# Opening of a two-layer kernel: tables fetched later, warm-up matmuls, an earlier T1, and the experts' table in two parts

## The reference

```python
gate = lora_add(einsum('bnh,fh->bnf', x, W_gate), x, A_gate, B_gate)   # F = 2752, rank 16, 16 adapters
up   = lora_add(einsum('bnh,fh->bnf', x, W_up),   x, A_up,   B_up)
act  = silu(gate) * up
y    = lora_add(einsum('bnf,hf->bnh', act, W_down), act, A_down, B_down)
logits = y @ W_gate + b_gate                       # 8 experts, other weights than above
_, top_idx = top_k(logits, 2)
out = x + mean(relu(einsum('bsd,edh->bseh', y, W_e) + b_e) taken at top_idx, over the two)
```

## Time and profile before

| | |
|---|---|
| median of 3 runs | 1841.7 us (1838.97 to 1843.03) |
| profiled execution, its time | 1838.5 us |
| its span | 1836.6 us |
| PE busy | 1808.3 us (98%) |
| DVE busy | 1255.6 us (68%) |
| ACT busy | 754.8 us (41%) |
| POOL busy | 1097.3 us (60%) |
| moved by DMA | 350.34 MB, mean 191 GB/s |

### The profile page before, as it was taken

How to read it: one execution, slowest core, us unless ns; L and a number is a source line. 1 busy time by engine, 2 the same in 40 slices (tenths; PEclk the granted TensorE clock), 3 DMA queues, 4 the chain that set the end, 5 groups by cost and what they waited for, 6 DMA issues and landing times. The chain is left out here.

```text
span 1836.6 us, 25207 instructions
## 1 busy us (share of the span) xinstructions
PE 1808.3 (98%) x8578; PEld 1505.3 (82%) x8578; DVE 1255.6 (68%) x1489; ACT 754.8 (41%) x1197; POOL 1097.3 (60%) x712
## 2 busy tenths in 40 slices
PE   8999999999999999999999999999999999999997
PEld 6788888888888888888888888888888888888886
DVE  7977887885567797888888886477798743234400
ACT  5544444443543335444443444443323333333332
POOL 3788888873444454446656543444434777777674
PEclk9999999999999999999999999999999999999999
DMA  6466566645577655555566565576635875567653
GB/s 227 161 232 222 207 205 224 240 138 172 194 247 245 220 186 169 189 179 180 189 205 210 187 205 191 192 255 221 223 109 188 246 195 149 145 188 194 150 104 48
DMA packets 128973, 350.34 MB, mean 191 GB/s; under 512 B 15296, under 2 KB 17216, under 8 KB 128576
## 3 DMA queue, kind: packets, MB, share of 16 engines
q1 hardware_dynamic: 110608, 286.92, 45.6%
q0 software_dynamic: 17952, 61.75, 14.1%
q10 hardware_dynamic: 288, 0.02, 0.0%
HBM read 267.49 MB, written 90.05 MB: 195 GB/s over the span
## 5 line engine op out<-in xcount | busy, mean ns | idle before, releaser
L1831 PE MATMUL PS<-R,ring 128*128 128x512 f32 (+1 forms) x1804 | 708.5, 393 | 11.0 <-DVE R L1022 8.4
L1832 PE MATMUL PS<-R,ring 128*128 128x512 f32 (+1 forms) x1804 | 704.0, 390 | 0.0
L1833 PE MATMUL PS<-R,ring 128*128 128x512 f32 (+1 forms) x1804 | 703.5, 390 | 0.0
L1831 PEld LDWEIGHTS PS<-R,ring 128*128 128x128 f32 x1804 | 339.7, 188 | 79.2 <-DVE ring L956 11.6
L1833 PEld LDWEIGHTS PS<-R,ring 128*128 128x128 f32 x1804 | 339.3, 188 | 71.8
L1832 PEld LDWEIGHTS PS<-R,ring 128*128 128x128 f32 x1804 | 339.8, 188 | 66.0
L824 POOL TENSOR_TENSOR ring<-raw,ring 128x1024 fp32r<-128x1024 f32 x78 | 192.2, 2464 | 268.9 <-ACT ring L963 268.8
L803 POOL DMA_INDIRECT brw<-in_bgu,idx_b x88 | 100.4, 1141 | 222.6 <-DVE R L1139 184.9
L1831 PE MATMUL PS<-ring,R 128*128 128x512 f32 x592 | 231.7, 391 | 1.7 <-DVE FT L1323 1.7
L1832 PE MATMUL PS<-ring,R 128*128 128x512 f32 x592 | 230.8, 390 | 0.0
L1833 PE MATMUL PS<-ring,R 128*128 128x512 f32 x592 | 230.4, 389 | 0.0
(11 more groups left out here) (192 smaller groups left out, 2391.0 us busy)
## 6 DMA issues: line engine op xcount, KB each, us to landing
raw<-in_wp SPq DMA_DIRECT2D x122, 512.0 KB, 4.4
act_scratch<-FT SPq DMA_DIRECT2D x140, 256.0 KB, 4.9
FT<-act_scratch SPq DMA_DIRECT2D x70, 512.0 KB, 3.9
raw<-in_we SPq DMA_DIRECT2D x64, 512.0 KB, 5.6
ytp<-in_wgb SPq DMA_DIRECT2D x96, 256.0 KB, 4.7
raw<-wt_scratch SPq DMA_DIRECT2D x40, 512.0 KB, 4.4
out<-in_xn SPq DMA_DIRECT2D x17, 512.0 KB, 5.5
y_scratch<-FT SPq DMA_DIRECT2D x7, 1024.0 KB, 5.9
```

Source lines behind the costliest of these rows:

```text
L1831: e.matmul(out_, hi, whi, start=start, stop=False, skip_group_check=True)
L1832: e.matmul(out_, hi, wlo, start=False, stop=False, skip_group_check=True)
L1833: return e.matmul(out_, lo, whi, start=False, stop=stop, skip_group_check=True)
```

## The change

There are four edits.

1. `constants(e, False)`, the two small tables for the adapters' rows, is issued on SP after B11's quarters and no longer as ACT's first job; `adapter_rows` goes on DVE behind B11's low parts and no longer ahead of everything.
2. DVE fills a tile with two memsets (`warm_fill`) as its first job, and PE runs five plain float32 matmuls of 128x128 by 128x256 on it, whose result nobody reads, before its first product.
3. On ACT, `ag_hi` goes ahead of B22's high parts; on DVE, T1 and then `ag_lo` go ahead of B22's low parts.
4. `table` is called in two halves, with the first three steps of `products(1, ...)` between them, and `turn(2)` comes after 12 steps of block 1's products and no longer after 10.

```diff
-        act.add(-100, constants, False)
+        sp.add(-35.5, constants, False)
...
-            key = op(g, 0) + 0.2 if g else early(17.6)
+            key = op(g, 0) + 0.2 if g else early(15.0)
             act.add(key, ag_hi, g)
-            dve.add(key + 0.01 if g else early(18.0), ag_lo, g)
+            dve.add(key + 0.01 if g else early(15.5), ag_lo, g)
...
         for h in range(2):
-            dve.add(early(20.5 + 0.1 * h), x0_t1, h)
+            dve.add(early(15.1 + 0.1 * h), x0_t1, h)
...
+        def warm_fill(e):
+
+            v = tile(JK_T).rearrange("p (n o) -> p n o", o=2)
+            e.memset(v[:, :, 0:1], 1.37).then_inc(s_warm, 1)
+            e.memset(v[:, :, 1:2], -2.91).then_inc(s_warm, 1)
+
+        dve.add(-60, warm_fill)
...
-        dve.add(-50, adapter_rows)
+        dve.add(early(7.5), adapter_rows)
...
+            e.wait_ge(s_warm, 2)
+            for i in range(5):
+                e.matmul(PS[:, 7, 0:256], tile(JK_T)[:, 0:128], tile(JK_T)[:, 128:384], start=True, stop=True)
             for g in range(NG):
                 first_pairs(g)
...
-            def table():
-
-                for q in range(32):
+            def table(qs):
+                for q in qs:
...
-                m.then_inc(s_rk, 1)
+                if q == 31:
+                    m.then_inc(s_rk, 1)
...
-            table()
+            table(range(16))
             begin(1, 8)
-            products(1, range(10))
+            products(1, range(3))
+            table(range(16, 32))
+            products(1, range(3, 12))
             turn(2)
-            products(1, range(10, 16))
+            products(1, range(12, 16))
```

More of the change, by code:

```diff
@@ L281, in build @@
         s_th, s_tl0 = sem("s_th"), sem("s_tl0")
+        s_warm = sem("s_warm")
         s_w0 = [sem("s_w00"), sem("s_w01")]
```

## The result

| | before | changed |
|---|---|---|
| median | 1841.55 us (5 runs, 1838.97 to 1843.03) | 1832.88 us (5 runs, 1832.45 to 1834.7) |
| ratio of times | | 0.9959, 95% interval [0.9947, 0.9971] |
| profiled execution, its time | 1838.5 | 1832.88 |
| its span | 1836.6 | 1831.1 |

The change is faster by 0.41% by that ratio, some 7.5 us. The forecast was 1839.9 with a range of 1836.8 to 1842.6: the direction was right, the size far too small. The spans of the two profiled executions differ by 5.5, those of the two copies by 6.8.

A forecast was written before the change was run, and what follows sets the result against it. The prediction took TensorE (PE) to be the path nearly from end to end, with DVE also pacing the opening. 0.7 us from the opening plus 1.1 from the table, 1.8, took 1841.7 to 1839.9, range 1836.8 to 1842.6.

The forecast's parts named there:

- item 1: Opening: adapters' table leaves the front of DVE's queue, PE starts about 0.5 us sooner; SP's extra issue costs nothing.
- Item 2: Opening: warm-up matmuls hidden at no cost; fast clock at PE's first product, a little likelier than not, saves PE 2.5 us.
- Item 3: Opening: POOL's first gather of the adapters' factors starts at about 10.5 instead of 7.34; all four in at 22.9.
- G: Opening: time when all four gathers of the adapters' factors are in; 22.9, allowed 21.5 to 23.5, 22.5 taken.
- Item 4: Opening, order on ACT and DVE: T2 starts at G + 11.15 against 34.37, and PE gets that shift, 0.7 us.
- the longer wait before the product at 50.3: Opening's end: sign that PE would wait longer than 1.14 us there, its other gains turning into waiting.
- Item 5: Experts' table: the 1.69 us wait goes, block 2 then waits 0.5; 1.1 us remain of 1.6.
- B: Opening: rival that PE paces it, so start and clock gains are kept; 4.1 us gained, 1837.6, chance 0.18.
- C: Opening: slower rival, POOL's second gather of B factors held as long as the first was; 1845.0, chance 0.08.
- D: Opening and block 2: rival that only waits move, block 2 late by the whole 1.7; 1841.4, chance 0.12.

The follow-up runs named there:

- the two copies: The kernel before and the changed kernel, each run once more with nothing altered; medians 1840.84 us and 1833.87 us.
- e6_spfirst: Kernel before with the two small tables issued as SP's very first transfers instead of on ACT; 1839.97 us, ratio 0.9998.
- the copy: The changed kernel run once more with all edits, for a second trace; 1833.87 us, ratio 0.9963.
- e2_warm: Kernel before plus only the warm-up (two memsets and five matmuls ahead of the first product); 1838.1 us, ratio 0.9987.
- e1_tables: Kernel before with only the small tables moved to SP and the adapters' row numbers behind B11's low parts; 1838.6 us, ratio 0.999.
- r_before: The kernel before run once more with no edit, for a second trace; 1840.84 us, ratio 1.0002.
- e8_order: Kernel before with only the new order of ag_hi, T1 and ag_lo ahead of B22's parts; 1841.88 us, ratio 1.0005.
- e4: Changed kernel without the five warm-up matmuls; 1836.48 us, ratio 0.9979.
- e10: Changed kernel with the experts' table in one piece again; 1837.48 us, ratio 0.998.
- e11: Changed kernel with adapter_rows on DVE behind two of B11's four low parts, not all four; 1834.2 us, ratio 0.9967.

## Why the prediction was wrong

The step that failed is item 1: the small tables' move was put at nothing for the transfers, and the first weight came 2.4 us earlier by it, which carried PE, the gathers and T2 with it. Two gains have no term in the sum at all: one in the middle of the kernel (1.05 to 1.8 us, cause open) and one in clock at the table (an estimated 0.9).

- **Item 1, the start: failed.** I put the gain at 0.5 us, from the queue of DVE alone, and moved the small tables at no cost or gain to the transfers. In fact the first weight lands 2.4 us earlier (3.44 against 5.80), and e6_spfirst shows the reason, the second queue. PE starts at 6.72 (6.09 in the copy), not near 7.9.
- **Item 2, the warm-up: right about its cost and about the bound.** Five products took 4.0 us and were hidden. The clock was there at the first product, 2.2 of the 2.5 us were gained over the first 12 products, and all of it was gone at 49.14. What I did not see is that it depends on the gap behind it (e2_warm) and so on item 1, and that the 2.5 is a price of one execution: without a warm-up 12 products are slow in before and e1_tables, but only 6 in r_before and 7 in e8_order.
- **Item 3, the gathers: mis-sized through item 1.** The first began at 9.08, not 10.5, because B11's low parts came that much sooner. "12.4 us after the first gather" nearly held (12.06, and 11.48 in the copy), so G was 21.14 (20.36 in the copy), below the range of 21.5 to 23.5 in both.
- **Item 4, T2 at G + 11.15: held.** 32.29 by that rule, 32.26 measured; in e4, e10 and e11 within 0.11 us. The copy, at G = 20.36, is at 31.93 and not 31.51. Neither the gathers nor PE hold it there: DVE works without a pause from B12's second low part on, which had waited for B12 to land, up to T2:

```profile
18.07 1.23 DVE L1011 TENSOR_TENSOR R<-X,R 128x1024 fp32r<-128x1024 f32 x1 [1.36 <-ACT R L1007]
...
31.93 2.36 DVE L1036 TENSOR_TENSOR FT<-FT 128x1024 f32<-128x1024 f32 x2
```

 Item 4 had T1 made in time in which DVE would wait anyway; with the gathers this early that time is used up, and earlier gathers bring nothing more. The opening gave 2.1 (2.4) instead of 0.7. That the shift of T2 is exactly what PE gets held in all 13 executions. Of the signs, the longer wait before the product at 50.3 did not come (1.01 after 1.14): what PE had gained beyond T2's shift went into the wait of 1.06 at the first adapter product.
- **Item 5, the table: nearly right in the profile, 1.55 for 1.1,** as block 2's wait was 0.17 and not 0.5: POOL's low part began 2.25 us behind the transposes as before (1406.27 and 1404.02), and block 2's first product followed 3.93 us behind them, where I had 4.15 for the first half alone. What I missed is the fall of the clock that this wait brings in some executions, an estimated 0.9 us in the mean.
- **The middle: not in the sum at all.** The changed kernel gains another 1.8 us between 49 and 305 us (its copy 1.05). There ACT waits for a gather of factors B to land, the copy out of PSUM (L1194) stands behind it on ACT, and PE waits for that. Before, ACT at one such place:

```profile
298.06 0.91 POOL L803 DMA_INDIRECT brw<-in_bgu,idx_b  x1 [0.30 <-issue]
303.90 0.63 ACT L1134 ACTIVATE R<-brw 96x512 fp32r<-96x512 f32 x1 [4.29 <-DMA brw<-in_bgu,idx_b]
```

 and in the changed kernel:

```profile
295.24 0.92 POOL L804 DMA_INDIRECT brw<-in_bgu,idx_b  x1 [0.30 <-issue]
299.96 0.63 ACT L1135 ACTIVATE R<-brw 96x512 fp32r<-96x512 f32 x1 [3.18 <-DMA brw<-in_bgu,idx_b]
```

 From issue to use it is 5.84 us in the one and 4.72 in the other, and PE's waits for that copy are 3.7 us in all before (2.5 and 1.2) and 2.2 after (1.5 and 0.7). From 49 to 305 us the profiles with warm-up gain 1.05 to 1.8 us on the kernel before in six of seven cases (0.6 in e11_rows); the six without are between 0.8 slower and 0.6 faster. That goes with the 2.6 us that e4_nowarm lacks, of which it explains 1 to 1.8, and with the gain of e2_warm. Why a warm-up at the start should make gathers 250 us later land sooner is open; it was not tried further, and with one or two profiles for each kernel the link itself rests on 14 executions.

Together, against the profiled kernel before: 2.1 to 2.4 from the opening, 1.55 from the table, 0.9 of clock, 1.05 to 1.8 from the middle: 5.6 to 6.7 against a measured 6.3. Against the mean of the executions without the edit in question it is 1.8, 1.55, 0.9 and 1.65, in all 5.9. My sum had 1.8.

Of the rivals, B came closest with its time (1837.6), but not by its mechanism: the gathers were nearly as early as it asked (21.14 and 20.36, where it asked for near 20) and PE was 3 us ahead, but it kept 2.1 to 2.4 of that, since DVE and not PE paced the opening. C did not come. In the changed kernel POOL's first gather of the factors B took 0.92 us, not 5.84 as in the earlier trace rows, and the second started at 27.08, so neither was held. In the copy the first was held nevertheless:

```profile
25.83 4.71 POOL L804 DMA_INDIRECT brw<-in_bgu,idx_b  x1 [11.79 <-DMA ad_scratch<-ytp]
```

 The second was not (0.91), T2 was the earliest of all, and nothing was lost. A hold of 4.7 to 6.1 us of this first gather stands in ten of the fourteen profiles, among them e1_tables (6.02), and not in the changed kernel, e4, e10 and e11. These four have edits 1 and 3 in common, but so has the copy; the cause was not tested. D's price at block 2 was 0.17.

## What to carry to other kernels

A chain that ends a stage (here T2 on DVE) tells what an earlier start is worth; follow it by the same instruction in every run, and take a second profile of the kernel before, since this one moved by 0.9 us. A warm-up gave the first real products the fast clock with gaps of 0.15 to 1.24 us behind it and not with 3.07; but here the end of the opening did not move by it, and what it gained in the time came later, unexplained. A wait of a microsecond or two in the middle of dense products can cost as much again in clock. Leave the first large transfer alone on the DMA engines: two tiny loads on another queue delayed it by 2.4 us.

## What the runs showed of the hardware

- A plain float32 product of 256 columns is recorded as two matmuls; five of them took 3.9 to 4.6 us, partly or wholly at the slow clock (at that pace each of the two takes 0.43 us, as long as a product of 512 columns). That agrees with the estimate of 4.3 made from the Trainium skill's four passes (FP8 and Floating Point Precision, TensorE Precision Notes), though the clock changed on the way.
- The granted clock came down to 1.2 GHz after an idle stretch of 3.07 us (e2_warm), but also after one of 1.7 us in three of the eight profiles that have it, and in two profiles after two waits close together (0.96 and 0.73, 0.62 and 0.72 us). Each such fall behind the start cost 1.6 to 1.7 us.
- At the start, with no warm-up, the clock came up after 6 to 12 slow products in seven executions. The Trainium skill (TensorE: Matmul & The Clock Gate, Part 1) ties the clock to how busy TensorE has been and says that the point of change varies from run to run; these executions agree.
- Two small loads on a second DMA queue beside the first weight made it land 5.05 us after its issue; ahead of it or behind it on the same queue, 2.9 and 2.7.
